# The layer norm inside the second attention: centring folded into ScalarE's square and scaling

## The reference

```python
h2 = jnp.einsum('bnk,dk->bnd', z, Wo)
out2 = _gat_layer(h2, mask[None], bo)
z2 = jax.nn.leaky_relu(out2, negative_slope=0.2)
mu = jnp.mean(z2, axis=-1, keepdims=True)
var = jnp.mean(jnp.square(z2 - mu), axis=-1, keepdims=True)
out = (z2 - mu) * jax.lax.rsqrt(var + LN_EPS) * gamma + beta
...
x = x + _L1_gnn_ref(h, adj, ...)
h = jnp.maximum(_layernorm(x, axis=-1), 0.0)
```

## Time and profile before

| what | value |
|---|---|
| median of 3 runs | 1673.04 us (1667.5 to 1674.67) |
| profiled execution, its own time | 1676.99 us |
| its span in the trace | 1675.2 us |
| granted TensorE clock, mean | 0.856 of full |
| DVE busy | 1235.5 us (74%) |
| PE busy | 1106.5 us (66%) |
| POOL busy | 1011.4 us (60%) |
| ACT busy | 843.4 us (50%) |

### The profile page before, as it was taken

The page is one execution under the profiler, slowest core; times in us unless marked ns, Lnnn a source line. Parts: engine busy times, 40 slices in busy tenths (PEclk is TensorE's granted clock), DMA queues, the critical chain, the costliest instruction groups (busy, mean ns, idle before and its releaser), DMA issues.

```text
span 1675.2 us, 14804 instructions
## 1 busy us (share of the span) xinstructions
PE 1106.5 (66%) x3605; PEld 606.6 (36%) x3605; DVE 1235.5 (74%) x1580; ACT 843.4 (50%) x2746; POOL 1011.4 (60%) x965
## 2 busy tenths in 40 slices
PE   0146655644998997699999957466527767755473
PEld 0024322212554554345555522122114445542131
DVE  7889587986999999957787059789749867625462
ACT  1025535672666665456656625556755556533131
POOL 2123486516987885576876668878448745307881
PEclk9998777877999999799999988777757869867796
DMA  9851565412230221011110044523035423116765
GB/s 327 215 182 57 177 189 155 142 38 82 82 88 26 83 70 37 13 35 42 44 45 7 13 144 126 144 81 101 19 113 172 138 75 108 39 49 209 207 189 157
DMA packets 101566, 176.75 MB, mean 106 GB/s; under 512 B 47488, under 2 KB 56224, under 8 KB 99424
## 3 DMA queue, kind: packets, MB, share of 16 engines
q0 software_dynamic: 31472, 102.93, 21.2%
q1 hardware_dynamic: 67280, 72.13, 13.7%
q10 hardware_dynamic: 2720, 0.68, 0.2%
HBM read 145.78 MB, written 34.10 MB: 107 GB/s over the span
## 4 chain that ended last, share of the span: by engine, by line
PE 29%; DVE 27%; POOL 19%; issue 11%; ACT 6%; DMA 4%; SPq 1%; DVEq 0%; ACTq 0%; POOLq 0%
PE PS L1366 15%; POOL big L695 10%; DVE big L1798 6%; POOL big L722 4%; DVE big L1790 3%; ACT big L995 3%; PE PS L1282 3%; DVE big L1794 2%; PE PS L1391 2%; PE PS L1427 2%; DMA big<-in_adj 2%; PE PS L1378 2%; DVE big L1682 2%; PE PS L1302 2%; DVE big L1782 2%
## 5 line engine op out<-in xcount | busy, mean ns | idle before, releaser
L1366 PE MATMUL PS<-big,ident 128*128 128x512 f32 x1044 | 507.0, 637 | 90.3 <-POOL big L722 66.8
L995 ACT ACTIVATE big<-big 128x64 f32<-128x64 f32 x1496 | 372.2, 337 | 189.5 <-DVE big L1755 111.0
L722 POOL TENSOR_TENSOR big<-big 128x512 f32<-128x512 f32 x373 | 378.7, 1046 | 120.5 <-DVE big L1755 101.3
L1366 PEld LDWEIGHTS PS<-big,ident 128*128 128x128 f32 x1044 | 207.9, 205 | 338.0 <-issue 243.5
L1798 DVE TENSOR_REDUCE big<-big 128x32 f32<-128x2048 f32 (+4 forms) x126 | 297.7, 2363 | 4.3
L1352 PE MATMUL PS<-big,ident 128*128 128x512 f32 x348 | 184.1, 688 | 128.8 <-ACT big L995 66.1
L1790 DVE TENSOR_TENSOR big<-big,PS 128x2048 f32<-128x2048 f32 (+4 forms) x84 | 198.5, 2363 | 63.1 <-PE PS L1378 60.5
L695 POOL DMA_INDIRECT big<-tab,SI x142 | 173.0, 1218 | 95.2 <-issue 40.4
L1282 PE MATMUL PS<-ident,big 128*128 128x128 f32 x640 | 105.3, 296 | 153.9 <-DMA big<-h_rows 67.2
L695 POOL DMA_INDIRECT big<-h_rows,SI x142 | 137.8, 971 | 51.1 <-issue 27.5
L1282 PEld LDWEIGHTS PS<-ident,big 128*128 128x128 f32 x640 | 84.1, 153 | 213.8 <-issue 84.8
(11 more groups left out here) (180 smaller groups left out, 1621.5 us busy)
## 6 DMA issues: line engine op xcount, KB each, us to landing
big<-in_adj SPq DMA_DIRECT2D x16, 1024.0 KB, 7.5
tab<-big SPq DMA_DIRECT2D x64, 132.0 KB
big<-tab SPq DMA_DIRECT2D x32, 264.0 KB
h_rows<-big SPq DMA_DIRECT2D x32, 256.0 KB
big<-h_rows SPq DMA_DIRECT2D x32, 256.0 KB
big<-in_x SPq DMA_DIRECT2D x16, 256.0 KB, 5.1
big<-xs SPq DMA_DIRECT2D x4, 1024.0 KB, 8.9
h_table<-big SPq DMA_DIRECT2D x16, 256.0 KB
```

Of the source, the lines that this page charges most:

```text
L722: ins = pool.tensor_tensor(bd(wbuf[:, i % NWB, j, :]), bd(rows[:, k + j, :]), over_d(S[:, h, k + j, :], B), ALU.mult)
L995: ins = act.activation(to, row, ACT.Copy, scale=S[:, h, k + j, b:b + 1])
L1366: mm = pe.matmul(to, ident[:, :], wbuf[:, i % NWB, k, :], start=(u != 2 and c == 0 and k == 0), stop=(c == len(parts) - 1 and k == n - 1))
```

## The change

GpSimd no longer makes a centred row. The mean is stored with a minus sign. ScalarE squares `no` with that as bias, 8 instructions of 64 columns for one of 512, and each gives its sum as an accumulator output, so VectorE's sum of squares goes away. The scaling becomes `Identity` with the reciprocal root as scale and `nshift`, minus mean times reciprocal root, as bias. VectorE makes `nshift` (128x8) right after `divide`. ScalarE's logarithm and exponential stand ahead of its `weigh`.

```diff
                 def finish2(m):
...
-                    t = m - 3
-                    if 0 <= t < NT:
-                        pool.wait_ge(z_mean, t + 1)
-                        pool.tensor_tensor(bd(no[:, t % 4, :]), bd(no[:, t % 4, :]),
-                                           over_d(ln[:, 0, (t % 2) * B:(t % 2 + 1) * B], B), ALU.subtract)\
-                            .then_inc(z_centred, 1)
...
                 for m in range(NT + 10):
-                    weigh(2, m - 1, 0)
                     t = m - 4
...
                         act.activation(ln[:, 1, v], ln[:, 3, v], ACT.Exp, scale=-0.5).then_inc(z_rooted, 1)
-                        act.wait_ge(z_rooted, t + 1)
+                    weigh(2, m - 1, 0)
+                    if 0 <= t < NT:
+                        act.wait_ge(z_shift, t + 1)
                         for b in range(B):
                             part, i = no[:, t % 4, b * D:(b + 1) * D], (t % 2) * B + b
-                            ins = act.activation(part, part, ACT.Copy, scale=ln[:, 1, i:i + 1])
+                            ins = act.activation(part, part, ACT.Identity, scale=ln[:, 1, i:i + 1],
+                                                 bias=nshift[:, i:i + 1])
                         ins.then_inc(o_scaled, 1)
                     t = m - 3
                     if 0 <= t < NT:
-                        act.wait_ge(z_centred, t + 1)
-                        if t >= 2:
-                            act.wait_ge(z_var, t - 1)
-                        act.activation(na[:, t % 2, :], no[:, t % 4, :], ACT.Square).then_inc(z_squared, 1)
+                        act.wait_ge(z_mean, t + 1)
+                        for b in range(B):
+                            i = (t % 2) * B + b
+                            ins = act.activation(na[:, t % 2, b * D:(b + 1) * D], no[:, t % 4, b * D:(b + 1) * D], ACT.Square,
+                                                 bias=ln[:, 0, i:i + 1], accum_out=ln[:, 2, i:i + 1])
+                        ins.then_inc(z_var, 1)
                     norm(2, m - 6)
...
-                    t = m - 3
-                    if 0 <= t < NT:
-                        dve.wait_ge(z_squared, t + 1)
-                        tell(dve.tensor_reduce(ln[:, 2, (t % 2) * B:(t % 2 + 1) * B], bd(na[:, t % 2, :]), AX.X, ALU.add),
-                             z_var, t + 1)
...
-                        tell(dve.tensor_scalar(mean, mean, 1.0 / D, None, ALU.mult), z_mean, t + 1)
+                        tell(dve.tensor_scalar(mean, mean, -1.0 / D, None, ALU.mult), z_mean, t + 1)
...
                         divide(u, m - 1)
+                        t = m - 4
+                        if u == 2 and 0 <= t < NT:
+                            v = slice((t % 2) * B, (t % 2 + 1) * B)
+                            dve.wait_ge(z_rooted, t + 1)
+                            if t >= 2:
+                                dve.wait_ge(o_scaled, t - 1)
+                            tell(dve.tensor_tensor(nshift[:, v], ln[:, 0, v], ln[:, 1, v], ALU.mult), z_shift, t + 1)
```

More of the change, by code:

```diff
@@ L262, in program @@
         ln = sb("ln", [P, 4, 2 * B])
+        nshift = sb("nshift", [P, 2 * B])
         epsc = sb("epsc", [P, 1])
@@ L389, in program @@
         z_rooted = sem("z_rooted")
+        z_shift = sem("z_shift")
         x_final = sem("x_final")
```

## The result

The changed kernel takes 1675.35 us (1671.59 to 1680.53), the kernel before 1672.1 us beside it: a ratio of 1.0024 [1.0014, 1.0035], or +4.0 us. The same kernel timed twice more gave 1.0024 [1.0008, 1.0039] and 1.0015 [1.0003, 1.0027]. It is slower, by 2.5 to 4 us (0.15 to 0.24%), where +8 was forecast. In the profiled executions (1671.59 us, span 1669.8) the change itself accounts for +1.9 us, counted from unit 2's first product to unit 3's: 267.8 us for 265.9 (267.77 and 265.91). The rest of the span doesn't hold the change, and over the fourteen profiles of this case it lies between 1399.9 and 1409.5 us, so spans are not compared here.

A forecast was written before the change was run, and what follows sets the result against it. Unit 2 was taken as bound by GpSimd early, a loop through GpSimd, ScalarE and VectorE in the middle, and ScalarE busiest in the tail. Gains 6.5, losses 14.1: about +7.7 us on 1673, forecast 1681, range 1667 to 1695.

The forecast's parts named there:

- the forecast's own case: Unit 2: ScalarE's queue becomes the bound from tile 9 on, 1674 to 1688 us; chance 0.55.
- 1 early: Early unit 2, GpSimd the bound: all five centrings vanish from a queue that never idles, -5.0 us.
- 2 step of tile 7: Step bound by VectorE, which makes scores of the 13-row tile while GpSimd then waits for `divide`: -0.5 us.
- 3 tile 8: Step weighing tile 8: ScalarE's rows, scaling and squares, 11.7 us, stay under GpSimd's 12.3, so -1.0 us.
- 4 tile 9: Step weighing tile 9: ScalarE becomes the bound, 9.82 us until L956, then 6.09: 15.91, so +2.4 us.
- 5 tiles 10 to 13: Four middle steps: ScalarE reaches L956 at 7.89 instead of 7.36; 13.98 against 13.45 us each, +2.1 us.
- 7 tile 15 to the ReLU: Tile 15's step up to the ReLU: 7.89 + 3.02 = 10.91 us against 9.37, so +1.5 us.
- 8 next ReLU: Tail: scaling waits for `nshift` behind L1855 to L1857 on VectorE; 11.55 us against 8.69, +2.9 us.
- 9 to L952 at 1220.91: Rest of the tail to old L956: another 11.55 us, small instructions and scaling, 14.92 against 11.32, +3.6 us.
- rival of cheap pairs: ScalarE: second pointer free (0.24 us), square with accumulator read at 0.32; -6.1 us, or 1667; chance 0.17.
- lost the port: VectorE's `nshift`, with two SBUF inputs, is blocked by GpSimd's weighings at each N: +26 us, or 1699; chance 0.10.
- Full gain: GpSimd's chain sets the end everywhere, so 16 times 1.0 us goes: 1657; chance 0.05.

The follow-up runs named there:

- padded: Changed kernel with an extra one-column ScalarE instruction behind each of a tile's first seven squares: 1682.35 us, ratio 1.0060 to the kernel before.
- one pointer: Changed kernel scaling by Copy with the scale operand alone, leaving out the shift by the mean: 1669.13 us, ratio 0.9983 to the kernel before.
- no accumulator: Changed kernel without accumulator outputs on the squares, VectorE's reduction given back: 1669.48 us, ratio 0.9985 to the kernel before.
- split squares: Changed kernel with four of each tile's eight squares moved behind the softmax exponential: 1665.99 us, ratio 0.9964 to the kernel before.
- hoist alone: Kernel before with only ScalarE's logarithm and exponential moved ahead of its weighing: 1671.18 us, ratio 0.9997 to the kernel before.
- early alone: Changed kernel with the new form for tiles 0 to 5 only, old form after: 1666.26 us, ratio 0.9971 to the kernel before.
- late alone: Changed kernel with the old form for tiles 0 to 5, new form for 6 to 15: 1679.15 us, ratio 1.0039 to the kernel before.
- t < 13: Changed kernel with the old form for tiles 13 to 15: 1668.06 us, ratio 0.9979 to the kernel before.
- combined: Changed kernel with four squares a tile behind the softmax exponential and the old form for tiles 13 to 15: 1659.31 us, ratio 0.9926 to the kernel before.
- t < 15: Changed kernel with four squares a tile behind the softmax exponential and new form up to tile 14: 1664.4 us, ratio 0.9954 to the kernel before.
- again: Changed kernel, no edit, second timing and profile: 1675.89 us, ratio 1.0024 to the kernel before.
- third: Changed kernel, no edit, third timing: 1673.98 us, ratio 1.0015 to the kernel before.

## Why the prediction was wrong in size

Its direction and its mechanism held; +8 was twice what the timing gave, and four times what unit 2 shows in the trace. The measured 1675.35 us lies inside the range of 1667 to 1695, and at the low edge of the 1674 to 1688 that I gave to the forecast's own case. The first sign of being wrong that I had named came true, since the pair's price of 0.33 us lies outside 0.35 to 0.5; with it the steps of tiles 10 to 13 take 13.3 us, not 14.0, and the tail's ReLUs stand 10.85 us apart, not 11.5. By its own steps, in us; the first line is the start of tile 7's step after unit 2's first product (94.9 before, 89.7 after), the others are from the timelines (the measured column is rounded by itself):

```
                              forecast   measured
1 early                         -5.0       -5.2
2 step of tile 7                -0.5       -0.5
3 tile 8 (19.42 -> 18.44)       -1.0       -1.0
4 tile 9 (13.51 -> 15.20)       +2.4       +1.7
5 tiles 10 to 13 (13.45->13.28) +2.1       -0.7
6 tile 14 (12.40 -> 13.26)      +1.6       +0.9
7 tile 15 to the ReLU           +1.5       +0.9
8 next ReLU (8.69 -> 10.85)     +2.9       +2.2
9 to L952 at 1220.91            +3.6       +3.0
sum                             +7.6       +1.2
```

The forecast's steps add up to 7.6; the prediction wrote 7.7, which changes nothing.

**The gains (1 to 3)** were right to 0.2 us each: GpSimd's queue without L736, then VectorE's without its reduction.

**The term that failed** is the price of a square with its accumulator's read, taken at 0.43 us as the middle between 0.32 and 0.54; it is 0.331. Seventy-two of them are 7.1 us too much. The second pointer went the other way, 0.331 for 0.315, 1.3 us too little over 80 scalings. Together: 7.6 - 7.1 + 1.3 = 1.8, where the trace shows 1.2 to the last step of the sum. Steps 4 to 9 are off by nearly this alone: their losses were put at 14.1, and 14.1 - 5.8 = 8.3 stands against 7.9 measured. Where the middle was chosen ("nothing favours an end"), the prediction had said itself that everything in ScalarE's queue overlaps what follows: an instruction of 334 ns there stands at intervals of 0.24 us, 0.09 less than it lasts. That was the nearest row, and it spoke for the low end. With the same 0.09 taken off, even the one-column row of 0.203 us gives an estimate of 0.24 + 0.11 = 0.35 for the pair.

**The rival of cheap pairs** had the pair nearly right (0.32) and would have been further off on the other side (-6.1): it tied to it a second pointer that costs nothing, where 80 x 0.09 = 7.2 us were to be paid. Two prices that have nothing to do with each other should not have been moved to their low ends together.

**The loop** follows one line in all kernels. L952's start after N, and the step that follows, from the timelines of steps with eight of ScalarE's instructions at their head:

```
kernel            L952 after N   step    difference   who is last at L952
before                7.36       13.45      6.09      GpSimd
padded                7.87       13.93      6.06      ScalarE's queue
changed               7.23       13.29      6.06      ScalarE's queue
one pointer           6.49       12.54      6.05      ScalarE's queue
no accumulator        6.48       12.54      6.06      ScalarE's queue
split squares         6.36       12.44      6.08      GpSimd
```

The 6.09 that the prediction took from the earlier trace rows holds to 0.04 us. In the changed kernel the wait for GpSimd ahead of this instruction is gone, as forecast.

**`nshift`** never lost the port: L1898's mean is 167 ns over all 16, so that rival is out. In the tail ScalarE waits for it as computed. **Full gain**: the forecast's condition, L952 by N + 6.4, was met only by the kernel with split squares.

**Behind the sum's last step** another 0.7 us is lost before unit 3 starts. From L956 or L952 to the start of the last eight scalings both kernels take 9.6 us. What follows is the store of the last rows, their reading back, and TensorE's first instruction on them. Before and after:

```profile
1234.97 2.02 ACT L969 ACTIVATE big<-big,stats 128x64 f32<-128x64 f32 x8
...
1242.22 1.12 PE L1282 MATMUL PS<-ident,big 128*128 128x128 f32 x4 [37.65 <-DMA big<-h_rows]
```

```profile
1230.48 2.02 ACT L965 ACTIVATE big<-big,stats 128x64 f32<-128x64 f32 x8
...
1238.39 1.11 PE L1282 MATMUL PS<-ident,big 128*128 128x128 f32 x4 [43.28 <-DMA big<-h_rows]
```

That is 7.25 us for 7.91. It repeats: 7.1 to 7.3 in the kernel before, the hoist alone, early alone, late alone, `t < 13` and the combined kernel, 7.65 with `t < 15`, 7.9 to 8.2 in the others. Late alone has the changed kernel's whole tail and takes 7.3, so the order of work in the tail isn't the cause, which stays open.

**All runs side by side**, as differences from the kernel before, in us; "timed" is what the ratio gives of 1672 us:

```
kernel            to the last scaling   to unit 3   timed
changed                 +1.2              +1.9      +4.0
again                   +1.2              +2.1      +4.0
third                   +1.3              +2.0      +2.5
early alone             -5.8              -5.9      -4.8
late alone              +6.7              +6.7      +6.5
no accumulator          -4.2              -3.3      -2.5
padded                  +7.0              +7.6     +10.0
one pointer             -6.3              -5.5      -2.8
split squares           -6.9              -6.3      -6.0
hoist alone             -0.3              -0.3      -0.5
t < 13                  -4.7              -4.5      -3.5
combined               -10.9             -11.0     -12.4
t < 15                  -9.5              -9.1      -7.7
```

**Open.** The changed kernel's timings give +4.0, +4.0 and +2.5 us, the trace of unit 2 +1.9 to +2.1. Two of the three intervals hold 2.0; the first begins at 2.3. In the table the timed value and that to unit 3 lie up to 2.7 us apart, to either side, so whether the change loses 1 or 2 us more elsewhere can't be told. The two mis-sized prices explain 5.8 of the 6.4 us between the forecast and the trace (7.6 and 1.2); if the timed +4.0 is right, about 2 us of it are in no term of the sum.

## What to carry to other kernels

On an in-order queue the price of added work is its time from start to start, and only where it stands ahead of something that others wait for: moving four squares a tile from one place to another was worth 8 us here. If an engine's rows stand closer together than they last, price an unseen instruction there as overlapped too, and don't take the middle of two bounds when the nearest row favours one of them. Ask stage by stage which engine is last before moving work off it: here the move paid where GpSimd was last, and cost where ScalarE was.

## What the runs showed of the hardware beyond that

VectorE's small instructions got shorter without an edit to them. In the changed kernel GpSimd's arithmetic ends earlier against VectorE's queue. The two groups of small instructions with two SBUF inputs (SBUF is the memory on the core), in the middle of unit 2 of the kernel before (1117 to 1190 us):

```profile
L1744 DVE TENSOR_TENSOR big<-big,mx 128x40 f32<-128x40 f32 (+1 forms) x6 | 4.5, 751 | 0.2
L1739 DVE TENSOR_TENSOR big<-big,SI 128x40 f32<-128x40 f32 (+1 forms) x6 | 3.7, 611 | 0.2
```

and of the changed kernel (1105 to 1180 us):

```profile
L1739 DVE TENSOR_TENSOR big<-big,SI 128x40 f32<-128x40 f32 (+1 forms) x6 | 2.4, 407 | 0.2
L1744 DVE TENSOR_TENSOR big<-big,mx 128x40 f32<-128x40 f32 (+1 forms) x6 | 1.7, 286 | 0.2
```

Together that is 0.67 us a step (751 + 611 - 407 - 286 ns). In the earlier trace rows L706 runs from 1136.13 to 1137.18, and L1744, begun at 1136.53 in the same timeline, ends at 1137.24, when L706 is over. In the changed kernel L1744 starts at 1139.09 and takes 0.20 us, although GpSimd has issued an indirect DMA at 1138.89: in the first step L1744 ended with GpSimd's arithmetic, in the second the DMA issue didn't hold it up. L1716, which has one tensor input, went from 0.17 to 0.35 us in the same step; why is not shown. So the kernel without accumulator, whose VectorE queue is 12.54 us a step, would by an estimate have had 12.54 + 0.67 - 0.18 = 13.03 with the durations of before, close to the 13.1 expected of it: a queue's length measured in one arrangement isn't that of the next.
